# A GNN and mixture-of-experts kernel: squares on ScalarE, the first layer's bias on VectorE, and the turn of the next tile moved behind the second layer's products

## What is computed

```python
xf = layernorm(x)                       # mean and variance of each row of 512
probs = softmax(xf @ Wr + br)           # 8 experts
vals, idx = top_k(probs, 2)
cw = (one_hot(idx, 8) * vals[..., None]).sum(axis=1)
for e in range(8):                      # summed over e
    h = relu(xf @ W1[e] + b1[e])
    out += cw[:, e] * (h @ W2[e] + b2[e])
x = x + out
```

## Time and profile before

| what | value |
|---|---|
| median of 3 runs | 2559.18 us (2556.94 to 2559.37) |
| the profiled execution, its own time | 2556.38 us |
| its span, first to last instruction | 2554.8 us |
| granted TensorE clock, mean | 0.999 of full speed |
| PE busy | 2511.1 us (98%) |
| DVE busy | 1899.3 us (74%) |
| ACT busy | 1486.9 us (58%) |
| POOL busy | 1045.2 us (41%) |

### The profile page before, as it was taken

The page is one execution under the profiler, slowest core; times in us unless marked ns, Lnnn a source line. Parts: engine busy times, 40 slices in busy tenths (PEclk is TensorE's granted clock), DMA queues, the critical chain, the costliest instruction groups (busy, mean ns, idle before and its releaser), DMA issues.

```text
span 2554.8 us, 40284 instructions
## 1 busy us (share of the span) xinstructions
PE 2511.1 (98%) x9906; PEld 1633.6 (64%) x9906; DVE 1899.3 (74%) x5059; ACT 1486.9 (58%) x3471; POOL 1045.2 (41%) x1293
## 2 busy tenths in 40 slices
PE   8999999999999999999999999999999999999999
PEld 4444455555488875555468885555547888888887
DVE  5555555556599976555589995557749999999997
ACT  2222245555288865555458885555525666666665
POOL 3222245555244435555333333555533333333332
PEclk9999999999999999999999999999999999999999
DMA  4444468888245448888635556998842334432331
GB/s 148 132 132 132 129 213 263 270 264 270 95 165 165 165 158 278 267 273 264 219 106 165 165 165 234 329 317 263 265 149 83 100 103 142 166 103 93 101 102 63
DMA packets 208171, 460.91 MB, mean 180 GB/s; under 512 B 34895, under 2 KB 35207, under 8 KB 208004
## 3 DMA queue, kind: packets, MB, share of 16 engines
q0 software_dynamic: 64928, 207.55, 27.9%
q1 hardware_dynamic: 73812, 125.17, 13.9%
q10 hardware_dynamic: 69264, 126.12, 13.4%
HBM read 245.32 MB, written 213.93 MB: 180 GB/s over the span
## 4 chain that ended last, share of the span: by engine, by line
PE 94%; DVE 2%; DMA 1%; ACT 1%; issue 1%; ACTq 0%; POOL 0%; DVEq 0%; SPq 0%; POOLq 0%
PE psY L679 11%; PE psM L793 9%; PE psY L793 9%; PE psH L793 9%; PE psY L693 6%; PE psY L701 6%; PE psY L710 6%; PE psT L659 5%; PE psS L805 4%; PE psS L806 4%; PE psY L881 3%; PE psH L915 3%; PE psH L928 3%; PE psH L919 3%; PE psY L893 3%; PE psY L884 3%
## 5 line engine op out<-in xcount | busy, mean ns | idle before, releaser
L565 POOL DMA_INDIRECT rows<-y_rows,lists x471 | 492.0, 1045 | 462.4 <-PE psS L806 341.5
L1341 DVE TENSOR_TENSOR lows<-rows,highs 128x512 fp32r<-128x512 f32 x471 | 325.9, 692 | 355.0 <-ACT highs L962 346.5
L962 ACT ACTIVATE outs<-psS 128x512 f32<-128x512 f32 x471 | 279.5, 593 | 275.4 <-PE psS L806 270.4
L962 ACT ACTIVATE highs<-rows 128x512 fp32r<-128x512 f32 x471 | 294.8, 626 | 145.1 <-ACT outs L962 103.0
L805 PE MATMUL psS<-highs,sel 128*128 128x512 f32 x471 | 346.8, 736 | 10.4 <-ACT outs L962 8.0
L572 POOL DMA_INDIRECT rows<-sum_rows,nodeI x158 | 210.8, 1334 | 314.5 <-DVE rows L1349 299.5
L679 PE MATMUL psY<-wy,res 128*128 128x512 f32 x632 | 286.1, 596 | 0.0
L962 ACT ACTIVATE outs<-psY 128x512 f32<-128x512 f32 x237 | 141.8, 599 | 231.1 <-PE psY L679 221.1
L793 PE MATMUL psM<-wz,res 128*128 128x512 f32 x544 | 255.6, 592 | 0.0
L793 PE MATMUL psY<-wz,res 128*128 128x512 f32 x536 | 251.7, 592 | 0.0
L793 PE MATMUL psH<-wz,res 128*128 128x512 f32 x528 | 248.0, 592 | 0.0
(11 more groups left out here) (204 smaller groups left out, 4915.0 us busy)
## 6 DMA issues: line engine op xcount, KB each, us to landing
sum_rows<-outs ACTq DMA_DIRECT2D x471, 256.0 KB, 3.8
y_rows<-outs SPq DMA_DIRECT2D x237, 256.0 KB, 2.0
rows<-in_x POOLq DMA_DIRECT2D x78, 256.0 KB, 3.2
outs<-in_x SPq DMA_DIRECT2D x78, 256.0 KB, 2.6
out_rows<-res SPq DMA_DIRECT2D x78, 256.0 KB, 2.0
rows<-y_rows,lists POOLq DMA_INDIRECT x471, 4.3
z_rows<-res SPq DMA_DIRECT2D x13, 512.0 KB, 5.5
res<-z_rows SPq DMA_DIRECT2D x13, 512.0 KB, 3.9
```

Of the source, the lines that this page charges most:

```text
L565: pool.indirect_dma_start(out=rows[:, t % RING, :], out_offset=None, in_=y_d, in_offset=bass.IndirectOffsetOnAxis(ap=col(srcT, t), axis=0) ...
L962: act.activation(o, i_, ACT.Copy).then_inc(signal, 1)
L1341: dve.tensor_tensor(lows[:, t % RING, :], rows[:, t % RING, :], highs[:, g, :].bitcast(F32), ALU.subtract)\
```

## The change

Per tile of the expert stage:

- PE drops the b1 matmul of `up_across`; `x_turn(k + 1)` is issued behind `down_parts(k - 2)`.
- DVE drops bn_stats, bn_aggr and the add of epsilon with two of the memsets. The last addition of the row becomes a scalar_tensor_tensor with an accumulator output, the sum of the row. DVE takes over `up_wide(k)`, as (psY times the scale) plus b1, from ACT. `finish(k - 3)` goes behind `h_parts(k - 2)`.
- ACT gets `squares(k + 1)`, a Square with the negative mean as bias and an accumulator output, loses `up_wide`, and does `norm(k + 1)` behind `gated(k - 1)` and `widen_down(k - 2)` ahead of `x_top(k + 1)`.
- POOL makes the negative mean ahead of `gates(k)`, then the variance (one more instruction), the power and the shift, which now come behind `gather_own(k + 4)`.
- The set-up of the split bias (six DVE instructions in the third graph layer) is gone.

```diff
@@ gpsimd
+            def negative_mean(k):
+                s, n = k % 2, k // 2
+                pool.wait_ge(var_in[s], uses(s) + n + 1)
+                pool.tensor_scalar(st[:, s, MEAN:MEAN + 1], st[:, s, XSUM:XSUM + 1], -1.0 / D, None, ALU.mult)\
+                    .then_inc(mean_in, 1)
+
             def scale_shift(k):
                 s, n = k % 2, k // 2
-                rstd(n, s, 1)
+                pool.wait_ge(square_in, k + 1)
+                pool.tensor_scalar(st[:, s, VAR:VAR + 1], st[:, s, XSQ:XSQ + 1], 1.0 / D, EPS, ALU.mult, ALU.add)\
+                    .then_inc(variance_in, 1)
+                pool.wait_ge(variance_in, k + 1)
+                pool.tensor_tensor(st[:, s, RSTD:RSTD + 1], st[:, s, VAR:VAR + 1], half, ALU.pow)\
+                    .then_inc(rstd_in[s], 1)
...
             for k in range(NT):
+                if k + 2 < NT:
+                    negative_mean(k + 2)
                 gates(k)
+                if k + 4 < NT:
+                    gather_own(k + 4, var_in, 1)
                 if k + 2 < NT:
                     scale_shift(k + 2)
-                if k + 4 < NT:
-                    gather_own(k + 4, var_in, 1)
@@ tensor
-                pe.matmul(psY[s][:, :], twos[:, :], b1s[:, :], start=False, stop=True, skip_group_check=True)\
-                  .then_inc(y_ps[s], 1)
+                mm.then_inc(y_ps[s], 1)
...
                 router(k)
                 up_parts(k)
-                if k + 1 < NT:
-                    x_turn(k + 1)
                 if k == 2:
                     pe.wait_ge(b2_back, 16)
                 if k >= 2:
                     down_parts(k - 2)
+                if k + 1 < NT:
+                    x_turn(k + 1)
                 up_across(k)
@@ scalar
+            def squares(k):
+                s, n = k % 2, k // 2
+                act.wait_ge(mean_in, k + 1)
+                act.activation(rows[:, 2 + s, :], kept(place(k)), ACT.Square, bias=st[:, s, MEAN:MEAN + 1],
+                               accum_out=st[:, s, XSQ:XSQ + 1]).then_inc(square_in, 1)
...
                 if k + 1 < NT:
-                    norm(k + 1)
+                    squares(k + 1)
                 if k >= 1:
                     gated(k - 1)
+                if k + 1 < NT:
+                    norm(k + 1)
                 exps(k)
-                up_wide(k)
+                if k >= 2:
+                    widen_down(k - 2)
                 if k + 1 < NT:
                     x_top(k + 1)
-                if k >= 2:
-                    widen_down(k - 2)
@@ vector
+            def up_wide(k):
+                s, n = k % 2, k // 2
+                dve.wait_ge(ll_ps, (LAYERS - 1) * NT + k + 1)
+                dve.scalar_tensor_tensor(psY[s][:, :], psY[s][:, :], 1.0 + 1.0 / STEP, b1row, ALU.mult, ALU.add)\
+                   .then_inc(wide[s], 1)
...
                     dve.tensor_reduce(stat(LOWEST), gate(LG), AX.X, ALU.min).then_inc(lg_sb[s], 1)
+                    up_wide(k)
...
                     after(k_q)
-                    k_x = step(dve.tensor_tensor(own_x, q, v, ALU.add))
+                    dve.scalar_tensor_tensor(own_x, q, 1.0, v, ALU.mult, ALU.add, accum_out=stat(XSUM))\
+                       .then_inc(var_in[s], 1)
...
-                if ahead:
-                    after(k_x)
-                    carry(2)
-                    k_bn = step(dve.bn_stats(stat(STAT, 6), own_x))
...
-                    k_var = step(dve.bn_aggr(stat(MEAN, 2), stat(STAT, 6)))
-                if ahead:
-                    after(k_var)
-                    variance(s)
...
             for k in range(NT):
+                if k >= 2:
+                    h_parts(k - 2)
                 if k >= 3:
                     finish(k - 3)
-                if k >= 2:
-                    h_parts(k - 2)
```

More of the change, by code:

```diff
@@ L113, in build @@
         LG, EX, TOP, CW, HIGH, LOW = (X * k for k in (0, 1, 2, 3, 4, 6))
+        XSUM, XSQ = 0, 1
         STAT, MEAN, VAR, RSTD, SHIFT, LOWEST, SUM, INV, IDX, TOPW = 0, 6, 7, 8, 9, 10, 11, 12, 13, 15
@@ L135, in build @@
         wg2 = nc.alloc_sbuf_tensor_at("wg2", [P, C, 2 * X], F32R, offset=res_at + 48 * D)
[L136 to L139, removed]
+        b1row = res[:, 13, :]
         down_raw = nc.alloc_sbuf_tensor_at("down_raw", [P, C, D], F32, offset=res_at + 56 * D)
@@ L290, in build @@
         pad_set = sem("pad_set")
+        mean_in = sem("mean_in")
+        square_in = sem("square_in")
+        variance_in = sem("variance_in")
         block = ctx.enter_context(nc.Block())
@@ L457, in make_room @@
                 load_w(down_raw, W2.rearrange("e f d -> (e f) d"), ex_in)
-                load_row(b1raw, b1.rearrange("e f -> (e f)"), ex_in)
+                load_row(b1row, b1.rearrange("e f -> (e f)"), ex_in)
             for l in range(LAYERS):
@@ L616, in gather_own @@
                                         bounds_check=ZERO).then_inc(node_in[s], 16)
+            def negative_mean(k):
[3 more added lines that the diff above has]
+                    .then_inc(mean_in, 1)
             def scale_shift(k):
                 s, n = k % 2, k // 2
-                rstd(n, s, 1)
+                pool.wait_ge(square_in, k + 1)
[4 more added lines that the diff above has]
+                    .then_inc(rstd_in[s], 1)
                 pool.wait_ge(rstd_in[s], uses(s) + n + 1)
-                pool.tensor_scalar(st[:, s, SHIFT:SHIFT + 1], st[:, s, MEAN:MEAN + 1], st[:, s, RSTD:RSTD + 1], -1.0,
-                                   ALU.mult, ALU.mult).then_inc(shift_in[s], 1)
+                pool.tensor_tensor(st[:, s, SHIFT:SHIFT + 1], st[:, s, MEAN:MEAN + 1], st[:, s, RSTD:RSTD + 1], ALU.mult)\
+                    .then_inc(shift_in[s], 1)
             def gates(k):
@@ L642, in _ @@
             gather_own(1, xn_ready, LAYERS)
+            negative_mean(0)
             scale_shift(0)
             gather_own(2, var_in, 1)
+            negative_mean(1)
+            gather_own(3, var_in, 1)
             scale_shift(1)
-            gather_own(3, var_in, 1)
             for k in range(NT):
+                if k + 2 < NT:
+                    negative_mean(k + 2)
                 gates(k)
+                if k + 4 < NT:
+                    gather_own(k + 4, var_in, 1)
                 if k + 2 < NT:
                     scale_shift(k + 2)
-                if k + 4 < NT:
-                    gather_own(k + 4, var_in, 1)
         @block.tensor
@@ L893, in up_across @@
                     mm = pe.matmul(psY[s][:, :], xcs[:, s, q * P:(q + 1) * P], up_cross[:, q, :],
-                                   start=False, stop=False, skip_group_check=True)
-                pe.matmul(psY[s][:, :], twos[:, :], b1s[:, :], start=False, stop=True, skip_group_check=True)\
-                  .then_inc(y_ps[s], 1)
+                                   start=False, stop=(q == C - 1), skip_group_check=True)
+                mm.then_inc(y_ps[s], 1)
             def hidden_turn(k):
@@ L936, in _ @@
             all_turns(pe, z_sb, LAYERS)
-            pe.wait_ge(ex_set, 2 * C + 3)
+            pe.wait_ge(ex_set, 2 * C + 1)
             for k in range(NT):
@@ L1072, in exps @@
                    .then_inc(p_sb[s], 1)
-            def up_wide(k):
+            def squares(k):
                 s, n = k % 2, k // 2
-                act.wait_ge(ll_ps, (LAYERS - 1) * NT + k + 1)
-                act.activation(psY[s][:, :], psY[s][:, :], ACT.Copy, scale=1.0 + 1.0 / STEP).then_inc(wide[s], 1)
+                act.wait_ge(mean_in, k + 1)
+                act.activation(rows[:, 2 + s, :], kept(place(k)), ACT.Square, bias=st[:, s, MEAN:MEAN + 1],
+                               accum_out=st[:, s, XSQ:XSQ + 1]).then_inc(square_in, 1)
             def gated(k):
@@ L1110, in _ @@
             act.wait_ge(pad_set, 2)
+            squares(0)
             norm(0)
@@ L1421, in split_small @@
                    .then_inc(ex_set, 1)
[L1422 to L1428, removed]
             def split_half(raw, high_, low_, cross_, q, again):
@@ L1534, in experts @@
                     dve.tensor_copy(stat(IDX, 2), smi[:, 0:2]).then_inc(top_set, 1)
-                if ahead:
-                    after(k_bn)
-                    carry(3)
-                    k_var = step(dve.bn_aggr(stat(MEAN, 2), stat(STAT, 6)))
-                if ahead:
-                    after(k_var)
-                    variance(s)
             def finish(k):
```

## The result

The changed kernel took 2534.64 us in the median of 4 runs (2531.82 to 2537.42), the kernel before 2558.75: a ratio of 0.991, 95% interval 0.9898 to 0.9922. It is faster by 24 us, and the forecast, 2547.5 with a range from 2540.0, was wrong: the sign was right, the size, 11 us, half of what came.

The account below looks back on a forecast made before the run. DVE was taken to pace the expert stage at 7.91 us a tile, PE needing 7.89. 75 tiles x -0.16 = -12.0, last tiles -0.5, start +0.9: -11.6 us, 2544.8 profiled, 2547.6 median; range -8 to -15 us.

Parts of the forecast that it names:

- What bounds the kernel: Expert stage before the change: DVE sets the pace at 7.91 us a tile, PE alone would need 7.89.
- PE: Expert stage: without the b1 matmul, 0.23 us, PE alone needs 7.66 us a tile; moved transposes cost the same.
- DVE: Expert stage, per tile: -0.84 removed, +0.58 up_wide, +0.02 last addition, +0.08 accumulator read; sum -0.16, so 7.75 us.
- the term for the accumulator's read: Reading out the last addition's accumulator on DVE: 0.08 us a tile, possibly nothing, or 0.19 if it waits.
- DVE stays the pacer: Expert stage after the change: DVE at 7.75 us a tile covers PE at 7.66 and still sets the pace.
- rival B: PE sets the pace if the accumulator read is free: DVE 7.67, PE 7.66, gain 17.7 us, 2541.5; chance 10%.
- Rival A: DVE's accumulating addition runs at half rate, pitch 1.22 for 0.61: +0.45 us a tile, +34 us, 2593; chance 8%.
- PSUM operands: up_wide on DVE reads and writes PSUM at no extra cost, 0.61 us of pitch; the skill's page adds 0.065.
- Rival C: The accumulator read on DVE waits for the addition, 0.19 us: only -0.05 a tile, -3.4 us, 2555.8; chance 12%.
- Rival D: The POOL and ACT chain sets the pace: norm and exps end late, DVE stops at the reciprocal; chance 8%.
- The start: First tile of the expert stage: DVE idles 0.9 us as up_wide waits for L884; counted once, +0.9 us.

## Why the prediction was wrong

**What bounds the kernel: right.** DVE at 7.91 with PE at 7.89 just under it; taking 0.23 from PE alone gave nothing.

**PE: right.** 7.66 was forecast, 7.64 measured; a fifth product costs 0.23.

**DVE: the step that failed is the term for the accumulator's read, and with it "DVE stays the pacer".** The terms removed came as forecast: FIND_INDEX8 to xls takes 0.27 us, 0.84 less. The forecast was -0.16 us a tile in all; DVE's own pace fell by 0.30, from 7.91 to 7.61. The read, taken at 0.08, cost nothing, and that alone, 6 us of DVE's time over 75 tiles, brings DVE level with PE. The price was taken from ACT's read, which costs 0.09 there, though the same text had zero as its lower end and named that case as rival B, at 10%. The rest, 0.06, is in small terms. From the reduce to L1530 there are 0.67 us in the early tiles (1952.85 - 1952.18), where 0.11 + 0.58 was forecast; L1530's own pitch and that of the last addition are 0.60, where 0.61 was used; and the list behind xls is 0.02 shorter. With DVE at 7.61, PE holds the pitch at 7.64, and with the one tile of 8.3 us the mean over 75 tiles is 7.649, against 7.907 before: 75 x 0.258 = 19.4 us for the 12.0 forecast.

**Rival B** is what happened: PE paces, "the gain is 18". Its 2541.5 stands for a gain of 17.7, and the profiled execution gained 19.0; the scatter of the medians did the rest, and the result fell outside the range, whose lower end was set tight on B. The sign that the forecast named for B, PE without any gap, is what the profile shows.

**Rival A, the accumulating addition at half rate: refuted.** L1540 has a pitch of 2305.93 - 2305.33 = 0.60 with two fp32 SBUF sources and the accumulator, no more than without. The sentence of the Trainium skill (Vector Engine (DVE) Microarchitecture Reference, section 7) doesn't hold for this instruction; the measurement decides.

**PSUM operands: right by the rows.** up_wide, which reads and writes PSUM, has a pitch of 2303.97 - 2303.36 = 0.61. The 0.065 us that the Trainium skill's errata table (VectorE: DVE Perf Modes) adds for a PSUM source don't show.

**Rival C: refuted** by the same rows as the read.

**Rival D** exists as a link and not as a pace: its one tile is the one of 8.3 us, 0.65 us in all. The shift came 1.1 us late there, and both slacks gave way: PE stood 0.45 us at the turn, and DVE stood at the reciprocal, which waits for exps behind norm:

```profile
2313.50 0.16 DVE L1535 RECIPROCAL st<-st 128x1 f32<-128x1 f32 x1 [0.61 <-ACT sm L1085]
```

So the reciprocal's slack was about 1.13 - 0.61 = 0.5 us, half of the 1.0 forecast, and that of x_turn 1.13 - 0.45 = 0.7 (0.4 by the forecast's own figures of 5.1 and 5.5). That the turn had to move was right. The price of leaving it was too high: the forecast had PE stopping 1.5 us a tile, and the run without the move lost 8.39 - 7.64 = 0.75, 1.4 at every second turn. That run's own expectation, 7.9 to 8.3, was too low.

**The start: one term missed, and the clock not foreseen.** Missed: the two rows that DVE prepares in front of the expert stage, `experts(-2)` and `experts(-1)`, lose bn_stats and bn_aggr too. They stood ahead of the third layer's last sums on DVE, for which PE idled 2.2 us; that idle time is gone: -2.3 us. In the kernel before, another order of the same work gave about the same. Not foreseen: the first tiles were forecast 0.9 us longer for up_wide's wait, and are 3.0 longer (23.7 us against 20.7). The wait is there, at 0.86 us in the first tile and, in the second, 2.52:

```profile
1920.44 0.70 DVE L1493 SCALAR_TENSOR_TENSOR psY<-psY,res 128x512 f32<-128x512 f32 x1 [0.86 <-PE psY L900]
...
1929.79 0.70 DVE L1493 SCALAR_TENSOR_TENSOR psY<-psY,res 128x512 f32<-128x512 f32 x1 [2.52 <-PE psY L900]
```

The second is long because PE ran at half its clock just then. The run with two tiny instructions more, which has up_wide in the same place and the full clock throughout, has 0.72 and 0.69:

```profile
1919.25 0.70 DVE L1493 SCALAR_TENSOR_TENSOR psY<-psY,res 128x512 f32<-128x512 f32 x1 [0.72 <-PE psY L900]
...
1926.09 0.70 DVE L1493 SCALAR_TENSOR_TENSOR psY<-psY,res 128x512 f32<-128x512 f32 x1 [0.69 <-PE psY L900]
```

Its first tiles take 21.2 us, 0.5 more than in the kernel before. So the wait costs no more than the 0.9 forecast, and about 2.5 of the 3.0 us belong to the clock (an estimate from these profiles). The window of 1919 to 1934 us in the changed kernel (granted clock 0.77), and in the run with up_wide later, where it was 1.00:

```profile
1919.00:1934.00 15.00, 11.41 (x48) 8.68 (x46) 10.54 (x38) 6.92 (x22) 4.83 (x11) 0.77 0.17 42
```

```profile
1919.00:1934.00 15.00, 11.71 (x63) 9.34 (x64) 13.35 (x49) 9.24 (x32) 7.38 (x16) 1.00 0.24 72
```

In the clock's own record of the first the granted clock was 0.5, the 1.2 GHz level, for 6.8 us from 1923.8 on; it fell within an idle time of PE of 1.83 us. In the run with two tiny instructions more PE idles 1.84 us at the same place, and in the run with up_wide later 2.07 us once, and neither has such a stretch there. Of the ten profiles of the changed kernel and its variants eight have one near the start of the stage; of the three of the kernel before and its variants one does. What brings a stretch in one execution and not in the next, and whether the change makes it more likely, stays open.

**The sum of the profiled execution:** -2.5 (up to the first router, 2.3 of it from the cause named) + 3.0 (first tiles) - 19.4 (75 tiles) - 0.2 (last tiles) = -19.1, against 2554.8 - 2535.6 = 19.2 between the spans. The forecast had -11.6; of the 7.5 us between, the pitch is 7.4, and the misses ahead of the stage and in its first tiles cancel but for 0.4, by luck. The other 3 to 5 us of the medians' difference are the scatter of executions, which goes in part with the mean granted clock. In the experiments the kernel before took 2557.0 us in the mean of 21 runs at 0.999 and 2559.7 in the mean of 8 at 0.997. Comparing medians with the forecast, the place of one profiled run within them was a term that I carried as fixed, and it wasn't.

## What to carry to other kernels

When two engines are within a fraction of a per cent of each other, neither's relief alone is worth more than that fraction, and both together are worth the smaller one's; compare the periods of both engines from start to start, and say which becomes the pacer for each end of each unknown price. If that changes within the bounds, the case beyond the switch needs more than a tenth of the chance. A chain made longer on idle engines was free here only because its consumer was moved too: check every waiter's slack, and look at the seams in front of the loop, where the same instructions stand with other neighbours.

## What the runs showed of the hardware

- A scalar_tensor_tensor of 128x512 fp32 with an accumulator output keeps its pitch of 0.60 us, and DVE's read of the accumulator, 0.08 us long, takes no pitch at all; ACT's read after a Square took 0.09 (2300.68 to 2300.77).
- ACT's Square of 128x512 has a pitch of 0.62 to its read:

```profile
2300.06 0.71 ACT L1092 ACTIVATE rows<-res,st 128x512 f32<-128x512 f32 x1
2300.68 0.18 ACT L1092 ACTIVATION_READ_ACCUMULATOR rows<-res,st 128x1 f32 x1
2300.77 1.67 ACT L1102 ACTIVATE outs<-psY,sm 128x64 f32<-128x64 f32 x8
```

- With a late producer up the chain, the loop of four engines settled into a rhythm of two tiles (7.73 and 9.25 us) and not into one longer pitch; one late gather moved it into another (8.36 and 8.14), which is shorter in the mean.
- The gather's issue on GpSimd, 0.54 us behind the instruction in front of it in the changed kernel, is about 1.67 us behind it once, at the same tile in each profile; in the kernel before that one is 1.56. What delays it was not tried.
- Short stretches at the 1.2 GHz level, 3.4 or 6.8 us long, came in the profiled executions at the starts of the second and third layers and of the expert stage, not at the same ones each time; one execution of the thirteen had none before its last microseconds. That they explain the 5 to 10 us by which executions of one kernel differ is not shown.
